# The bias of the second up projection: from a TensorE product to four fused VectorE passes

## The chip, the cores and the metric

The kernel runs on one core of one Trainium2 chip. The metric is the device time of one launch in microseconds, the median of several executions. Three executions of the kernel before took 1491.62, 1492.84 and 1496.29 us; the median is 1492.84 us.

## What is computed

The reference takes x, 8 batches of 512 tokens by 256 channels in fp32, normalises it, and adds to x the outputs of two branches that read the same normalised tokens. One is attention with 16 heads of 16 channels: compressed blocks of 16 tokens, the 4 best blocks of each query, and a window of 32 tokens, merged with a gate. The other is the one at issue here, a gated MLP with 1,024 hidden channels and, beside it, a mixture of 1,024 small experts:

```
mlp = silu(h @ Wg + bg) * (h @ Wu + bu) @ Wd + bd
return mlp + experts_states
```

The gate projection `h @ Wg + bg` is called g below, the second up projection `h @ Wu + bu` is called u. Both biases are random numbers of spread 0.7, in fp32.

## The kernel before

There are four stages, each a block in which the five engines run their own programs and meet at semaphores. The first (until about 24 us) loads weights and prepares them. The second (until about 185 us) normalises and projects all batches. The third, from 187.7 to 1438 us, holds nearly all of the time. The fourth adds the output projection and stores.

The third stage handles 32 units, a unit being one batch and one group of 4 heads. For the attention a unit covers all 512 tokens of its heads; for the MLP and the experts it covers 128 of the batch's 512 tokens. `steps` (a loop over pairs of units, then the last two by hand) calls `step(t)` on every engine. The order within a step is written out by hand for each engine, and the step of unit t already does the first part of unit n = t + 1: its query products, its best blocks and its expert scores. Only the last unit (the tail) has no n.

PSUM banks are dealt out as rings (class `Banks`): Q has two banks for query products (lc, p03, p00, p01, p13, p10, p11, p23, p20, p21, p33, p30, p31, m0, m1 in that order; p11 is head 1, row tile 1 of the n unit), K three banks, F two banks (w0, w1, sim, g0, u0, g1, u1, t0, t1), Y one. A job can be written once the job two places ahead of it in a ring of two has been read. So p11 waits until p13 has been read, and p21 until p23 has been.

Around the change, TensorE's step has this order. `token_rows` gives w0, w1 and sim (line 1625). `up_rows` (lines 1607 to 1620) makes the hidden channels for 128 tokens, transposed: 4 slices of 128 channels for each of g0, u0, g1 and u1. Ahead of the first slice of each job it multiplies the stationary `bias3` (96 rows, bf16) with `tile_of` (96x512, a pattern of ones) into the whole bank (line 1612); the fp32 bias stands in `bias3` as three bf16 terms, in rows 0 to 31, 32 to 63 and 64 to 95. The slices then accumulate on it (line 1617). g0 stands ahead of the four head rounds; then in rounds h = 0, 1, 2 one slice each of u0, g1 and u1 follows each of the four parts, interleaved with `queries(n, h, part)` (line 1635) and the key products. In round 3 come the four parts of `mlp_down` (line 1766), of which parts 0 and 2 wait until u0 and u1 have been read.

ScalarE turns g into a tanh (line 1275), and so w0 and w1; its exponentials are on lines 1241 and 1259. VectorE's step has this order: expert products (line 1495) and `expert_silu` (line 1506), `compressed`, `best_blocks` (line 1413), half of `selection` (line 1438), `gate(0)` (line 1378), the reductions of head 0's query products (`block_max`, line 1394), the other half of `selection`, `up(0)` (line 1385), `best_keys` (line 1467), the reductions of head 1, `key_marks` (line 1475), `gate(1)`, the reductions of head 2, `unselected` (line 1445), `best_pairs`, `up(1)`, the reductions of head 3, and then the local scores and the results. `best_blocks` hands over to GpSimd (line 1120), which hands back. GpSimd sums the expert weights (line 1175) and makes the table of score sums (line 1149).

`bias3` is prepared in the first stage: six small transfers on ScalarE's queue (line 410, three for each bias) into b1, and six VectorE passes (lines 392 to 397). SP loads the weights of the third stage at the end of the second (lines 563 to 567), the last being the bias bdb; behind it SP issues the first qf, kc and xt (line 573). TensorE and GpSimd begin the third stage with a wait for all of these weights (`units_in`).

Of the kernel before, what the change touches and what calls it, by code (L numbers as in the profile page):

```python
# [20 lines left out]
BF16 = mybir.dt.bfloat16  # L21
ALU = mybir.AluOpType
# [7 lines left out]
P = 128  # L30
# [5 lines left out]
FT = FF // P  # L36
# [116 lines left out]
def build(nc, x, Wq, Wk, Wv, Wo, Wck, Wcv, Wg, bg, Fg, fbg, Fu, fbu, Fd, fbd, Rq, keys, down, up, out):  # L153
# [16 lines left out]
    with outer:  # L170
# [11 lines left out]
        sb, ps, sem = make(outer)  # L182
# [11 lines left out]
        wfg = sb("wfg", [P, 2, FF])  # L194
        wfu = sb("wfu", [P, 2, FF])
# [3 lines left out]
        wsim = sb("wsim", [P, 2, 2 * PH * KEYS])  # L199


        bias3 = sb("bias3", [96, 2, 2, P], BF16)
        tile_of = sb("tile_of", [96, 4, P], BF16)
        bdb = sb("bdb", [P, C])
        wo = sb("wo", [P, 2, C])
        ar0 = sb("ar0", [P, TT, C])

        pad = sb("pad", [P, 12])
        units_in = sem("units_in")
# [4 lines left out]
        xt = sb("xt", [P, 2, 2, P])  # L214
# [4 lines left out]
        sb, _, _ = make(projecting)  # L219
# [41 lines left out]
        with inner:  # L261
            sb, ps, sem = make(inner)
# [4 lines left out]
            kn = sb("kn", [P, 2, P])  # L267
            kT = sb("kT", [64, 2, C])
            dn = sb("dn", [P, EX // P, C])
            b1 = sb("b1", [96, 2, 2, P])  # L270
            b2 = sb("b2", [96, 2, 2, P])
            b3 = sb("b3", [96, 2, 2, P], BF16)
            b4 = sb("b4", [96, 2, 2, P], BF16)
            bank = [ps(f"sbank{i}", [P, 512]) for i in range(4)]
            wq_in, rq_in, kn_in, dn_in = sem("wq_in"), sem("rq_in"), sem("kn_in"), sem("dn_in")
            wg_in, bias_in, proj_in = sem("wg_in"), sem("bias_in"), sem("proj_in")
            cleared = sem("cleared")
# [24 lines left out]
            @block.gpsimd  # L302
            def _(pool):
                ch = Chain(pool, pool_chain, 0)
                g = nc.gpsimd

                def keep(ap, pattern, base, cm, fill, op=ALU.is_ge):
                    ch.link(g.affine_select(out=ap, in_=ap, compare_op=op, fill=fill, base=base,
                                            pattern=pattern, channel_multiplier=cm))
                g.memset(eps[:, :], 1e-5)  # L310
                g.memset(b1[:, :, :, :], 0.0).then_inc(cleared, 1)
                for k, m in enumerate((ident, identb)):
                    ch.link(g.memset(m[:, :], 0.0))
                    g.affine_select(out=m[:, :], in_=m[:, :], compare_op=ALU.not_equal, fill=1.0, base=0,
                                    pattern=[[-1, P]], channel_multiplier=1).then_inc(identity, 1)
                    g.memset((wck, wcv)[k][:, :, :], 0.0).then_inc(cleared, 1)
                for m in (any_ok, head_rows):
                    g.memset(m[:], 1.0)
                ch.link(g.memset(quad_rows[:, :], 1.0))
                keep(any_ok[:, :], [[P, TT]], -BLK, 1, 0.0)  # L320
                for rows in (slice(0, 64), slice(64, 128)):
                    keep(head_rows[rows, :], [[-D, HG]], 0, 1, 0.0)
                    keep(head_rows[rows, :], [[D, HG]], D - 1, -1, 0.0)
                keep(quad_rows[:, :], [[-32, HG]], 0, 1, 0.0)
                keep(quad_rows[:, :], [[32, HG]], 31, -1, 0.0)
                g.memset(causal_ts[:, :], 0.0)
                ch.link(g.memset(causal_st[:, :], 0.0))
                keep(causal_ts[:, 0:64], [[-1, 64]], 0, 1, NEG)
                keep(causal_st[:, :], [[1, 64]], 0, -1, NEG)
# [52 lines left out]
            @block.vector  # L382
            def _(dve):
                ch = Chain(dve, dve_chain, 0)
                v = nc.vector
                statistics(dve, 0)
                dve.wait_ge(std_ready, 1)
                ch.link(v.reciprocal(rstd[:, 0, :], std[:, 0, :]))
                normalize(0)
                statistics(dve, 1)  # L390
                dve.wait_ge(bias_in, 6 * 16)
                ch.link(v.tensor_copy(b3[:, :, :, :], b1[:, :, :, :]))
                v.tensor_copy(bias3[0:32, :, :, :], b3[0:32, :, :, :])
                ch.link(v.tensor_tensor(b2[:, :, :, :], b1[:, :, :, :], b3[:, :, :, :], ALU.subtract))
                ch.link(v.tensor_copy(b4[:, :, :, :], b2[:, :, :, :]))
                v.tensor_copy(bias3[32:64, :, :, :], b4[32:64, :, :, :])
                v.tensor_tensor(bias3[64:96, :, :, :], b2[64:96, :, :, :], b4[64:96, :, :, :], ALU.subtract)
                statistics(dve, 2)
                statistics(dve, 3)
                dve.wait_ge(std_ready, 2)  # L400
                v.reciprocal(rstd[:, 1:4, :], std[:, 1:4, :])

            @block.scalar
            def _(act):
                for h in range(8):
                    act.dma_start(wg8[16 * h:16 * h + 16, :], Wg).then_inc(wg_in, 16)
                act.wait_ge(cleared, 1)
                for r in range(3):
                    for a, src in enumerate((fbg, fbu)):
                        act.dma_start(b1[32 * r:32 * r + 4, a, :, :],  # L410
                                      src.rearrange("(j k p) -> k j p", j=2, k=4)).then_inc(bias_in, 16)

                def copy(dst, src, **kw):
                    return nc.scalar.activation(dst, src, ACT.Copy, **kw)
                deviation(act, 0, 1)
                for i, job in enumerate(jobs):
                    b = bank[i % 4]
                    act.wait_ge(pe_full, i + 1)
                    if job[0] == "wqT":
                        last = copy(wqT[:, job[1], :], b[:, 0:C])  # L420
                    elif job[0] == "rqT":
                        last = copy(rqT[:, 2 * job[1]:2 * job[1] + 2, :], b[0:64, :].rearrange("p (k n) -> p k n", k=2))
                    elif job[0] == "kT":
                        last = copy(kT[:, :, :], b[0:64, :].rearrange("p (k n) -> p k n", k=2))
                    elif job[0] == "dn":
                        last = copy(wdn[:, job[1], job[2] * 512:job[2] * 512 + 512], b[:, :])
                    elif job[0] == "wgate":
                        last = copy(wv[:, :, C:C + 3], b[:, 0:8].rearrange("p (a n) -> p a n", a=2)[:, :, 0:3], scale=1.0 / H)
                    else:
                        last = copy(wsim[:, job[1], :], b[:, :])  # L430
                    last.then_inc(read, 1)
                deviation(act, 1, 4)
# [3 lines left out]
        with inner:  # L436
# [69 lines left out]
            def _(sp):  # L506
# [55 lines left out]
                for i in range(B - 4, B):  # L562
                    t = Turn(i // 2, i % 2, tail=(i == B - 1))
                    step(t, None if t.tail else t.next())
                    for dst, src in lots[i]:
                        sp.dma_start(dst[:, :, :], src.rearrange("(a p) n -> p a n", p=P)).then_inc(units_in, 16)
                sp.dma_start(bdb[:, :], fbd.rearrange("(o n) -> o n", o=1).broadcast_to([P, C])).then_inc(units_in, 16)
                for name in ("xt", "qf"):
                    sems, per = by_half[name]
                    sp.wait_ge(sems[0], per * (B // 2 + 1))  # L570
# [312 lines left out]
        with inner:  # L883
# [116 lines left out]
            def hidden(j):  # L1000
                return hT[:, 4 * j:4 * j + 4, :].rearrange("p f t -> p (f t)")
# [90 lines left out]
            def _(pool):  # L1092
# [15 lines left out]
                pool.sem_inc(armed, 1)  # L1108
                pool.wait_ge(constants, 8)

                pool.wait_ge(units_in, 16 * 6)

                def pad_wait():

# [249 lines left out]
            def _(dve):  # L1364
# [16 lines left out]
                def up(t, j):  # L1381

                    F.wait_read(dve, t, f"g{j}")
                    F.wait_full(dve, t, f"u{j}")
                    F.released(f"u{j}", v.tensor_tensor(hidden(j), hidden(j),
                                                        F.bank(f"u{j}")[:, :], ALU.mult))

                def block_max(t, h, part):

# [211 lines left out]
            def _(pe):  # L1601
                mm, tr = nc.tensor.matmul, nc.tensor.transpose
                pe.wait_ge(armed, 1)
                pe.wait_ge(units_in, 16 * 6)
                pe.wait_ge(constants, 8)

                def up_rows(t, name, j, k):

                    w_, kind = (wfg, 0) if name == "g" else (wfu, 1)
                    if k == 0:  # L1610
                        F.wait_free(pe, t, f"{name}{j}")
                        mm(F.bank(f"{name}{j}")[:, :], bias3[:, kind, j, :], tile_of[:, :, :].rearrange("r k t -> r (k t)"),
                           start=True, stop=True)
                    o = P * (4 * j + k)
                    dst = F.bank(f"{name}{j}")[:, k * P:k * P + P]
                    for c in range(2):
                        last = mm(dst, w_[:, c, o:o + P], xt[:, t.half, c, :], start=False, stop=(c == 1),  # L1617
                                  skip_group_check=True)
                    if k == 3:
                        F.filled(f"{name}{j}", last)  # L1620
# [349 lines left out]
```

## Time and profile before

| | |
|---|---|
| median of 3 executions | 1492.84 us (1491.62 to 1496.29) |
| profiled execution, its own time | 1490.08 us |
| its span, first to last instruction | 1488.3 us |
| busy: TensorE matmuls | 1399.5 us (94%) |
| busy: TensorE weight loads | 1041.1 us (70%) |
| busy: VectorE | 1148.8 us (77%) |
| busy: ScalarE | 927.1 us (62%) |
| busy: GpSimd | 946.8 us (64%) |
| mean granted TensorE clock | 0.981 of full speed |

The profile is of one execution. In it PE is TensorE's matmuls, PEld its weight loads, DVE VectorE, ACT ScalarE, POOL GpSimd, SPq the queue of SyncE. A line of a timeline has the start and the length in us, the engine, the source line, the operation, what it writes and what it reads; in brackets stands how long the engine was idle just before, and which engine's work ended that. Lines that follow each other with the same work are merged (x4 is four instructions). Lengths of neighbours overlap, since one instruction begins while the one ahead still ends; what an instruction costs its engine is the distance from its start to the next one's.

### The profile page before, as it was taken

How to read it: one execution, taken by the hardware profiler on the slowest of the kernel's cores; microseconds unless marked ns; L12 is line 12 of the kernel's file. 1: busy time of each engine (PE TensorE's matmuls, PEld its weight loads, DVE VectorE, ACT ScalarE, POOL GpSimd, SP SyncE). 2: the span in 40 equal slices, each digit the busy share in tenths (PEclk: the TensorE clock that was granted, in tenths of full speed). 3: DMA queues.
4: the chain of work that ended last, by engine and by line, in shares of the span. 5: the costliest groups of instructions: out<-in, count | busy, mean ns of one | idle time of the engine just before them, and what ended most of it. 6: DMA issues, size and time to landing. Idle time of an engine off the chain costs nothing. (4 is left out here: it accounts for less than half of the span.)

```text
span 1488.3 us, 43616 instructions
## 1 busy us (share of the span) xinstructions
PE 1399.5 (94%) x14864; PEld 1041.1 (70%) x14960; DVE 1148.8 (77%) x4512; ACT 927.1 (62%) x1684; POOL 946.8 (64%) x877
## 2 busy tenths in 40 slices
PE   6899569999999999999999999999999999999978
PEld 4566437777777777777777777777777777777757
DVE  5444378888888888888888888888888888888712
ACT  3776436666666666666666666666666666666641
POOL 4655357777777766666666666666676666666720
PEclk8999969999999999999999999999999999999989
DMA  6556842211112222222212222122222222222027
GB/s 187 202 192 213 269 82 54 52 44 48 46 47 51 52 52 52 52 50 47 47 47 47 50 52 47 48 52 52 52 52 52 52 52 52 66 52 53 9 83 250
DMA packets 217149, 113.76 MB, mean 76 GB/s; under 512 B 128872, under 2 KB 211224, under 8 KB 217112
## 3 DMA queue, kind: packets, MB, share of 16 engines
q1 hardware_dynamic: 216304, 112.88, 27.9%
q10 hardware_dynamic: 808, 0.42, 0.2%
q8 instruction: 19, 0.31, 0.1%
q14 instruction: 18, 0.15, 0.0%
HBM read 73.08 MB, written 40.16 MB: 76 GB/s over the span
## 5 line engine op out<-in xcount | busy, mean ns | idle before, releaser
L1394 DVE TENSOR_REDUCE bmax<-q_bank 128x32 f32<-128x512 f32 (+3 forms) x512 | 221.2, 487 | 34.4 <-PE q_bank L1635 34.2
L1149 POOL TENSOR_TENSOR sumxy<-xy 128x1024 f32<-128x1024 f32 x128 | 246.1, 1942 | 0.0
L1241 ACT ACTIVATE pts<-k_bank 128x512 f32<-128x512 f32 (+2 forms) x384 | 177.4, 490 | 42.2 <-PE k_bank L1670 41.4
L1115 POOL TENSOR_TENSOR pad<-pad 128x1 f32<-128x1 f32 x32 | 6.2, 193 | 287.4 <-DVE top L1413 287.4
L1495 DVE SCALAR_TENSOR_TENSOR mw<-sumxy,c,ex 128x1024 f32<-128x1024 f32 x128 | 162.0, 1287 | 13.4 <-ACT ex L1259 9.6
L1617 PE MATMUL f_bank<-xt,wfu 128*128 128x128 f32 x1024 | 162.4, 281 | 0.0
L1635 PE MATMUL q_bank<-ko,qo 96*128 96x512 bf16 (+3 forms) x512 | 142.6, 306 | 16.9 <-DVE bmax L1394 16.7
L1175 POOL TENSOR_TENSOR cw<-cw,mw 128x1024 f32<-128x1024 f32 x64 | 150.9, 2358 | 11.5 <-ACT mw L1265 8.9
L1617 PE MATMUL f_bank<-xt,wfg 128*128 128x128 f32 x1024 | 150.3, 279 | 0.0
L1617 PEld LDWEIGHTS f_bank<-xt,wfu 128*128 128x128 f32 x1024 | 139.4, 191 | 11.5
L1318 ACT ACTIVATE oT<-k_bank 128x512 f32<-128x512 f32 x64 | 38.2, 597 | 173.8 <-PE k_bank L1685 129.3
L1265 ACT ACTIVATE mw<-mw,erec 128x1024 f32<-128x1024 f32 x128 | 145.7, 1139 | 0.0
L1259 ACT ACTIVATE ex<-sumxy,nmax 128x1024 f32<-128x1024 f32 x128 | 143.2, 1146 | 0.0
L1617 PEld LDWEIGHTS f_bank<-xt,wfg 128*128 128x128 f32 x1024 | 134.4, 191 | 8.3
L1766 PE MATMUL y_bank<-wfd,hT 128*128 128x256 f32 x512 | 136.0, 388 | 0.5 <-issue 0.5
L1780 PE MATMUL y_bank<-wup,cwT 128*128 128x256 f32 x512 | 124.4, 386 | 8.0 <-ACT cwT L1355 8.0
L1625 PE MATMUL f_bank<-wdn,xt 128*128 128x512 f32 x256 | 122.0, 599 | 0.0
L1309 ACT ACTIVATE qo<-k_bank 32x512 bf16<-32x512 f32 x128 | 75.4, 589 | 60.8 <-PE k_bank L1756 57.9
L1780 PEld LDWEIGHTS y_bank<-wup,cwT 128*128 128x128 f32 x512 | 92.1, 190 | 25.5 <-ACT cwT L1355 15.6
L1766 PEld LDWEIGHTS y_bank<-wfd,hT 128*128 128x128 f32 x512 | 87.2, 190 | 14.4 <-issue 0.7
L1670 PE MATMUL k_bank<-qo,ko 128*128 128x384 bf16 (+3 forms) x416 | 96.0, 280 | 0.0
L1275 ACT ACTIVATE sw<-f_bank 128x512 f32<-128x512 f32 x64 | 38.2, 597 | 79.1 <-PE f_bank L1625 79.0
(211 smaller groups left out, 3307.8 us busy)
## 6 DMA issues: line engine op xcount, KB each, us to landing
qo<-s_qs SPq DMA_DIRECT2D x192, 64.0 KB, 2.2
ko<-s_ks SPq DMA_DIRECT2D x186, 64.0 KB, 2.2
s_qs<-parts SPq DMA_DIRECT2D x8, 768.0 KB, 4.7
s_ks<-parts SPq DMA_DIRECT2D x8, 768.0 KB, 6.3
s_v<-vo SPq DMA_DIRECT2D x8, 544.0 KB, 3.0
vv<-s_v SPq DMA_DIRECT2D x32, 136.0 KB, 2.3
vw<-s_v SPq DMA_DIRECT2D x64, 68.0 KB, 2.5
xin<-in_L_attn_x_dram SPq DMA_DIRECT2D x8, 512.0 KB, 7.1
```

Source lines behind the costliest of these rows:

```text
L1149: done("sum_done", g_.tensor_tensor(sumxy[:, h, :, :], xy[:, 0, h, 0:XK, None].broadcast_to([P, XK, KEYS]), xy[:, 1, h, None, :].broadcast ...
L1175: done("cw_sum", g_.tensor_tensor(cw[:, :], mw[:, 0, :] if h == 1 else cw[:, :], mw[:, h, :], ALU.add))
L1241: last = s.activation(pts[:, h, OFFS[j]:OFFS[j] + n], bank[:, 0:n], ACT.Exp)
L1259: done("ex_done", s.activation(ex[:, h % 2, :], sumxy[:, h, :, :].rearrange("p a b -> p (a b)"), ACT.Exp, bias=nmax[:, h:h + 1]))
L1265: done("ms_done", s.activation(mw[:, h, :], mw[:, h, :], ACT.Copy, scale=erec[:, h:h + 1], accum_out=csm[:, h:h + 1]))
L1394: last = v.tensor_reduce(bmax[:, i, h, 0:n], Q.bank(job)[:, o:o + n * BLK].rearrange("p (n j) -> p n j", j=BLK), AX.X, ALU.max)
L1495: done("mw_done", v.scalar_tensor_tensor(mw[:, h, :], sumxy[:, h, :, :].rearrange("p a b -> p (a b)"), c8[:, h, 7:8], ex[:, h % 2, :], ALU ...
L1617: last = mm(dst, w_[:, c, o:o + P], xt[:, t.half, c, :], start=False, stop=(c == 1), skip_group_check=True)
L1625: last = mm(F.bank(job)[:, :], xt[:, t.half, c, :], w_[:, c, o:o + 512], start=(c == 0), stop=(c == 1))
L1635: last = mm(bank[:, o:o + n], qo[0:SP3, t.half, h, P * i:P * i + P], ko[0:SP3, t.half, h, 0:n], start=True, stop=(i > 0))
L1766: mm(Y.bank("y")[:, 0:C], hT[:, f, :], wfd[:, f, :], start=(f == 0), stop=False)
L1780: last = mm(Y.bank("y")[:, 0:C], cwT[:, e, :], wup[:, e, :], start=False, stop=(e == 7))
```

## The change

The bias of u is no longer a product of TensorE. `up_rows` issues the product of line 1612 for g alone, and for u the first slice product sets the start flag. The bias is kept as bias_u, 128 partitions by 8, one value for each hidden channel, and VectorE's `up(j)` adds it while it multiplies: four scalar_tensor_tensor passes of 128 columns, (bank + bias_u) * hT, take the place of one tensor_tensor pass of 512 columns. `bias3` and its four work tensors lose the half that held u's bias, and so three of the six transfers on ScalarE's queue go. bias_u is loaded by one transfer on SP's queue, behind bdb and ahead of qf, kc and xt, and `units_in` is waited for at 7 transfers instead of 6.

```diff
-        bias3 = sb("bias3", [96, 2, 2, P], BF16)
+        bias3 = sb("bias3", [96, 2, P], BF16)
+        bias_u = sb("bias_u", [P, FT])
...
-                dve.wait_ge(bias_in, 6 * 16)
-                ch.link(v.tensor_copy(b3[:, :, :, :], b1[:, :, :, :]))
+                dve.wait_ge(bias_in, 3 * 16)
+                ch.link(v.tensor_copy(b3[:, :, :], b1[:, :, :]))
...
                 for r in range(3):
-                    for a, src in enumerate((fbg, fbu)):
-                        act.dma_start(b1[32 * r:32 * r + 4, a, :, :],
-                                      src.rearrange("(j k p) -> k j p", j=2, k=4)).then_inc(bias_in, 16)
+                    act.dma_start(b1[32 * r:32 * r + 4, :, :],
+                                  fbg.rearrange("(j k p) -> k j p", j=2, k=4)).then_inc(bias_in, 16)
...
+                sp.dma_start(bias_u[:, :], fbu.rearrange("(f p) -> p f", p=P), allow_slow_non_contiguous=True).then_inc(units_in, 16)
...
-                pool.wait_ge(units_in, 16 * 6)
+                pool.wait_ge(units_in, 16 * 7)
...
                     F.wait_full(dve, t, f"u{j}")
-                    F.released(f"u{j}", v.tensor_tensor(hidden(j), hidden(j),
-                                                        F.bank(f"u{j}")[:, :], ALU.mult))
+                    for k in range(4):
+                        f = 4 * j + k
+                        last = v.scalar_tensor_tensor(hT[:, f, :], F.bank(f"u{j}")[:, P * k:P * k + P], bias_u[:, f:f + 1],
+                                                      hT[:, f, :], ALU.add, ALU.mult)
+                    F.released(f"u{j}", last)
...
-                pe.wait_ge(units_in, 16 * 6)
+                pe.wait_ge(units_in, 16 * 7)
...
-                    w_, kind = (wfg, 0) if name == "g" else (wfu, 1)
+                    w_ = wfg if name == "g" else wfu
                     if k == 0:
                         F.wait_free(pe, t, f"{name}{j}")
-                        mm(F.bank(f"{name}{j}")[:, :], bias3[:, kind, j, :], tile_of[:, :, :].rearrange("r k t -> r (k t)"),
+                    if k == 0 and name == "g":
+                        mm(F.bank(f"{name}{j}")[:, :], bias3[:, j, :], tile_of[:, :, :].rearrange("r k t -> r (k t)"),
                            start=True, stop=True)
...
-                        last = mm(dst, w_[:, c, o:o + P], xt[:, t.half, c, :], start=False, stop=(c == 1),
+                        last = mm(dst, w_[:, c, o:o + P], xt[:, t.half, c, :], start=(name == "u" and c == 0), stop=(c == 1),
                                   skip_group_check=True)
```

## Rows read from the trace of the kernel before

**Rows 1.** Busy time of each engine in stretches of the third stage: TensorE, weight loads, VectorE, ScalarE, GpSimd, clock, DMA
```profile
260.00:1380.00 1120.00, 1097.61 (x12671) 819.72 (x12759) 958.60 (x3882) 740.10 (x1405) 770.69 (x701) 1.00 0.21 50
716.94:734.46 17.52, 17.18 (x131) 13.90 (x132) 16.83 (x98) 15.43 (x32) 9.96 (x9) 1.00 0.17 32
```

**Rows 2.** Timeline of TensorE's matmuls, one unit (start us, length us, idle time ahead)
```profile
712.72 1.88 PE L1625 MATMUL f_bank<-wdn,xt 128*128 128x512 f32 x4
...
723.20 0.38 PE L1612 MATMUL f_bank<-tile_of,bias 96*128 96x512 bf16 x1
723.42 0.61 PE L1617 MATMUL f_bank<-xt,wfu 128*128 128x128 f32 x4
...
730.20 0.28 PE L1635 MATMUL q_bank<-ko,qo 96*128 96x256 bf16 x1 [0.23 <-DVE bmax L1394]
...
731.93 0.38 PE L1612 MATMUL f_bank<-tile_of,bias 96*128 96x512 bf16 x1
...
739.96 1.03 PE L1766 MATMUL y_bank<-wfd,hT 128*128 128x256 f32 x4
```

**Rows 3.** The same view, product p11 in an early and in a late unit
```profile
269.59 0.28 PE L1635 MATMUL q_bank<-ko,qo 96*128 96x256 bf16 x1 [0.24 <-DVE bmax L1394]
...
1152.56 0.28 PE L1635 MATMUL q_bank<-ko,qo 96*128 96x256 bf16 x1 [0.25 <-DVE bmax L1394]
```

**Rows 4.** Table of waits from 260 to 1380 us (us in total, times, longest)
```profile
PE q_bank L1635 <- DVE bmax L1394: 7.0, 29, 0.3
```

**Rows 5.** Timeline of TensorE's weight loads, product p21 of the same unit
```profile
734.50 0.10 PEld L1635 LDWEIGHTS q_bank<-ko,qo 96*128 96x128 bf16 x1 [0.15 <-DVE bmax L1394]
```

**Rows 6.** Timeline of ScalarE, the same unit
```profile
714.72 0.60 ACT L1275 ACTIVATE sw<-f_bank 128x512 f32<-128x512 f32 x1 [2.54 <-PE f_bank L1625]
```

**Rows 7.** Timeline of VectorE, the same unit
```profile
713.09 0.42 DVE L1528 SCALAR_TENSOR_TENSOR yo<-y_bank,xb 128x256 f32<-128x256 f32 x1 [0.89 <-PE y_bank L1780]
713.43 2.47 DVE L1495 SCALAR_TENSOR_TENSOR mw<-sumxy,c,ex 128x1024 f32<-128x1024 f32 x2
715.82 0.68 DVE L1506 SCALAR_TENSOR_TENSOR sw<-sw,f_bank 128x512 f32<-128x512 f32 x1
716.94 1.28 DVE L1495 SCALAR_TENSOR_TENSOR mw<-sumxy,c,ex 128x1024 f32<-128x1024 f32 x1 [0.44 <-ACT ex L1259]
...
727.84 0.69 DVE L1385 TENSOR_TENSOR hT<-hT,f_bank 128x512 f32<-128x512 f32 x1
728.45 0.22 DVE L1467 MAX8 t<-sim 128x8 f32<-128x64 f32 x1
...
729.47 1.67 DVE L1394 TENSOR_REDUCE bmax<-q_bank 128x32 f32<-128x512 f32 x4
...
733.76 1.68 DVE L1394 TENSOR_REDUCE bmax<-q_bank 128x32 f32<-128x512 f32 x4
...
738.00 0.67 DVE L1385 TENSOR_TENSOR hT<-hT,f_bank 128x512 f32<-128x512 f32 x1
...
740.05 0.76 DVE L1394 TENSOR_REDUCE bmax<-q_bank 128x8 f32<-128x128 f32 x2 [0.73 <-PE q_bank L1635]
```

**Rows 8.** Timelines of SP's queue and of TensorE where the third stage begins
```profile
179.78 1.26 SPq L567 DMA_DIRECT2D bdb<-in_L_ffn_bd_dram  x1
...
182.40 0.60 SPq L573 DMA_DIRECT2D xt<-s_xt  x1
...
187.68 2.04 PE L1728 MATMUL q_bank<-kc,qf 64*128 64x128 f32 x8 [11.68 <-DMA xt<-s_xt]
```

**Rows 9.** Timelines of VectorE and GpSimd, passes side by side
```profile
214.30 3.24 DVE L1495 SCALAR_TENSOR_TENSOR mw<-sumxy,c,ex 128x1024 f32<-128x1024 f32 x2 [0.89 <-issue]
...
735.35 1.97 DVE L1445 TENSOR_SCALAR unsel<-struck 128x512 bf16<-128x512 f32 x1
...
726.17 2.36 POOL L1175 TENSOR_TENSOR cw<-cw,mw 128x1024 f32<-128x1024 f32 x1
...
735.13 3.94 POOL L1149 TENSOR_TENSOR sumxy<-xy 128x1024 f32<-128x1024 f32 x2
```

More of the change, by code:

```diff
@@ L269, in build @@
             dn = sb("dn", [P, EX // P, C])
[L270 to L273, printed above, removed]
+            b1 = sb("b1", [96, 2, P])
+            b2 = sb("b2", [96, 2, P])
+            b3 = sb("b3", [96, 2, P], BF16)
+            b4 = sb("b4", [96, 2, P], BF16)
             bank = [ps(f"sbank{i}", [P, 512]) for i in range(4)]
@@ L310, in _ @@
                 g.memset(eps[:, :], 1e-5)
-                g.memset(b1[:, :, :, :], 0.0).then_inc(cleared, 1)
+                g.memset(b1[:, :, :], 0.0).then_inc(cleared, 1)
                 for k, m in enumerate((ident, identb)):
@@ L390, in _ @@
                 statistics(dve, 1)
-                dve.wait_ge(bias_in, 6 * 16)
-                ch.link(v.tensor_copy(b3[:, :, :, :], b1[:, :, :, :]))
[L393 to L397, printed above, removed]
+                dve.wait_ge(bias_in, 3 * 16)
+                ch.link(v.tensor_copy(b3[:, :, :], b1[:, :, :]))
+                v.tensor_copy(bias3[0:32, :, :], b3[0:32, :, :])
+                ch.link(v.tensor_tensor(b2[:, :, :], b1[:, :, :], b3[:, :, :], ALU.subtract))
+                ch.link(v.tensor_copy(b4[:, :, :], b2[:, :, :]))
+                v.tensor_copy(bias3[32:64, :, :], b4[32:64, :, :])
+                v.tensor_tensor(bias3[64:96, :, :], b2[64:96, :, :], b4[64:96, :, :], ALU.subtract)
                 statistics(dve, 2)
```

## The prediction

> **What bounds the kernel now.** I looked for the stage first. In the stretch of the third stage in which every unit is alike, TensorE's matmuls cover 1,097.6 of 1,120 us and VectorE is busy for 958.6, at a granted clock of 1.00, which is 2.4 GHz [rows 1]. Read alone, that says: TensorE is the bound, so a matmul taken away is time gained. The timeline of one unit shows how far that holds. The same small wait returns in every unit: the last query product of head 1 (p11) stands 0.23 to 0.25 us until VectorE has read a bank [rows 2, 3], and the table of waits counts it 29 times in 29 units, 7.0 us in all [rows 4]. From the first of these waits shown to the last are 23 units: (1152.56 - 269.59) / 23 = 38.39 us a unit [rows 3]. One product later in the same ring, p21, the weight load waits 0.15 us on VectorE again [rows 5].
>
> So I followed that wait backwards. TensorE writes w0 from 712.72 on; ScalarE, idle for 2.54 us until it comes, takes it at 714.72 [rows 2, 6]. VectorE waits 0.44 us for ScalarE's exponential at 716.94, and from there to the end of the reduction that frees p21's bank (733.76 + 0.69) it is busy for 16.83 of 17.52 us [rows 1, 7]; what is left is mostly one hand-over to GpSimd and back. In that stretch stand the first up product (727.84), the eight maxima behind it (728.45) and the reduction of p13 (729.47, four reductions), which frees the bank that p11 wants [rows 7]. **TensorE and VectorE run side by side from w0 to p21, and VectorE arrives last.** From p21 to the next w0 TensorE is alone the limit: VectorE itself idles there, 0.73 us ahead of the reduction at 740.05 [rows 7]. A unit is thus VectorE's half plus TensorE's half.
>
> **Part one, the bias product is gone (u0 and u1).** 2 in each of 32 units, 64 in all. Start to start it takes 723.42 - 723.20 = 0.22 us [rows 2]; its busy time is longer since matmuls overlap. 64 x 0.22 = 14.1 us if TensorE were the limit at both places. But both stand between w0 (712.72) and p21 (734.50): at 723.20 and at 731.93 [rows 2, 5]. There TensorE already arrives early and waits. What it saves is added to its waits at p11 and p21. I take 0 for the 31 units with a successor; the last has no query products and no such wait, and may give back 2 x 0.22 = 0.4 us. The start flag set on each 128 columns' first matmul instead adds no instruction.
>
> **Part two, the up product as four passes.** The one pass of 512 columns takes 728.45 - 727.84 = 0.61 us start to start [rows 7]. No row shows a pass of 128 columns with one operand in PSUM and a per-partition scalar, so I build it. The result pass (256 columns, same instruction, PSUM source, constant scalar) takes 713.43 - 713.09 = 0.34 us start to start; 256 columns at 0.96 GHz are 0.267, which leaves 0.07 fixed. The expert pass has a per-partition scalar and 1,024 columns: (715.82 - 713.43) / 2 = 1.195 us, less 1.067 for its columns is 0.128 [rows 7]. The scalar so seems to cost 0.055 more. A new pass is 0.133 + 0.07 + 0.055 = 0.26 us, four are 1.05 us, and **VectorE needs 0.44 us more for each up product**. Bounds: 4 x 0.20 = 0.81 if the scalar is free (+0.20), and 4 x 0.30 = 1.20 if each pass pays 0.04 more yet (+0.59). I take the middle value because the two rows it comes from are the same instruction.
>
> The Trainium skill (VectorE: DVE Perf Modes, section on the TRN2 errata) speaks against small tiles too: a pass pays its fixed latency each time, (N + 151) / 0.96 ns for an fp32 pass of N columns. Laid end to end that would be 4 x 291 - 691 ns = +0.47 us a product, an estimate from that page, and 0.9 us more over the kernel than my sum; the rows agree with the direction, but show the next pass starting before the last one's end.
>
> Where the two extra 0.44 us fall: the first (up of u0, at 727.84) lies ahead of the p13 reduction, inside VectorE's chain. Everything behind it moves by 0.44: p11, key marks, the reduction at 733.76, p21. This is paid whole, 31 x 0.44 = 13.6 us. The second (at 738.00) lies behind p21. Behind it wait the reduction of p33 and the second half of the down product (part 2, at 739.96), which reads its result; that product would be written at about 738.00 + 0.67 + 0.88 = 739.55 while part 2 itself has moved to 740.4, and VectorE's idle 0.73 us takes the rest [rows 2, 7]. Cost 0, with 0.8 us of cover; without that cover it would be another 13.6 us.
>
> **Part three, the prologue.** Three bias transfers fewer on ScalarE's queue and six VectorE conversions of half the width: all end before a wait for input data in the first 25 us, so 0 (at best -1 us). New is one transfer of bias_u, 1,024 single elements, issued on SP's queue between bdb and the first qf, kc and xt. The bdb issue took 1.26 us (179.78); xt was issued at 182.40 and TensorE's first product of the stage began at 187.68, after 11.68 us of waiting that ended with xt [rows 8]. Whatever the issue takes moves xt, and both TensorE and GpSimd also wait for bias_u itself. Nearest row: an issue like bdb's, +1.3 us; bounds 0 (the stage change hides it) and +5 (it lands late in a busy queue). I take 1.3. The Trainium skill (DMA: Bandwidth & Descriptors, Rules for kernel authors) says a transfer whose last dimension is not contiguous becomes one descriptor per element; no row here shows such a transfer.
>
> **Sum.** +13.6 + 1.3 - 0.4 = +14.5 us. The profiled execution took 1490.08 us, the median of the runs shown is 1492.84, 0.2% more; I add the sum to the median: **1507.3 us**, 1.0% slower. A difference below 0.3% (4.5 us) can't be told from none.
>
> **The rivals.**
> *A. TensorE is the bound after all.* Its 98% speaks for it, the wait in every unit against it: an engine that waits for another at p11 doesn't profit from work taken away before p11. It would give 1492.8 - 14.1 + 1.3 = 1480 us, faster. It decides if VectorE's chain has slack that the wait doesn't show, at least 0.44 us. Chance 0.07.
> *B. Half and half.* The p21 wait of 0.15 us is small, so the second bias product might still count, with VectorE's extra at its low bound: 31 x (0.20 - 0.22) + 1.3, about 0: 1493 to 1495 us. Chance 0.07.
> *C. GpSimd blocks the new passes.* VectorE does get stuck behind GpSimd: a 512-column pass over SBUF took 1.97 us at 735.35 beside a GpSimd product of 735.13, and the expert pass, which takes 1.19 elsewhere, took some 2.0 of the 3.24 at 214.30. The up product with one side in PSUM isn't held today: 0.67 to 0.69 us, at 727.84 beside GpSimd's sum from 726.17 to 728.53 [rows 7, 9]. The new passes read a second SBUF operand, the scalar. If that counts, the first pass waits 0.7 us and a later one for the next sum of 2.36: 31 x (0.7 + 0.44) = +35 us at least, 31 x 3.5 = +108 at most; 1529 to 1600 us. The Trainium skill (SBUF — State Buffer, Who interferes with whom) says a VectorE instruction with two SBUF inputs contends with a GpSimd one that reads SBUF; whether a [P, 1] scalar is such an input it doesn't say. Chance 0.06.
>
> **Numbers.** Forecast 0.80. Its own range: 31 x 0.20 = 6.2 and 31 x 0.59 = 18.3, with 0 to 5 us of prologue: 1499 to 1516. B lies just below, A and C outside; the range 1497 to 1517 leaves out a little under 2 in 10. Faster by over 0.3% 0.08, within 0.07, slower 0.85.
>
> **What would show each step.** Right: a new pass of about 0.34 us busy, 0.26 start to start; the p11 wait at 0.23 + 0.22 + 0.44 = 0.9 us and p21's at 0.15 + 0.22 = 0.37; 38.83 us a unit; VectorE's wait at 740.05 down from 0.73 to 0.3. Wrong: a unit shorter than 38.39 (A), up passes of unequal length beside GpSimd (C), a wait for u1's result at the down product's part 2, or TensorE's first product of the stage more than 5 us later. A clock below 1.00 with the longer waits would be a cost that I don't count.

## The result and the profile after

The changed kernel took 1506.61 us, the median of 4 executions (1504.32 to 1510.04), against 1492.23 us for the kernel before beside it: a ratio of 1.0097, 95% interval 1.0075 to 1.0119, which is 14.4 us or 1.0% slower. The forecast was 1507.3 us. The profiled execution has a span of 1508.3 us and is the slowest of the four, 1510.04 us; the others took 1504.32 to 1507.10. So the difference of the two profiled spans, 20.0 us, is not the measure of the change. In the traces, the stretch in which all units are alike is a better one.

TensorE in the changed kernel, by the timeline: the product p11 in an early, two middle and a late unit, and the work ahead of and behind u0's first slice (line 1622 is line 1617 of before, 1640 is 1635, 1678 is 1673).

```profile
276.83 0.28 PE L1640 MATMUL q_bank<-ko,qo 96*128 96x256 bf16 x1 [1.01 <-DVE bmax L1398]
...
704.49 0.28 PE L1640 MATMUL q_bank<-ko,qo 96*128 96x256 bf16 x1 [0.82 <-DVE bmax L1398]
...
735.80 0.19 PE L1678 MATMUL k_bank<-causal_st,identb 128*128 128x64 bf16 x1
735.83 0.69 PE L1622 MATMUL f_bank<-xt,wfu 128*128 128x128 f32 x4
736.36 0.38 PE L1640 MATMUL q_bank<-ko,qo 96*128 96x512 bf16 x1
...
743.37 0.28 PE L1640 MATMUL q_bank<-ko,qo 96*128 96x256 bf16 x1 [0.91 <-DVE bmax L1398]
...
1171.00 0.28 PE L1640 MATMUL q_bank<-ko,qo 96*128 96x256 bf16 x1 [0.81 <-DVE bmax L1398]
```

From the first to the last are 23 units: (1171.00 - 276.83) / 23 = 38.88 us a unit, where it was 38.39 [rows 3]. The wait at p11 has grown from 0.24 us to 0.81 or 0.82 in every second unit and 0.90 to 0.92 in the others (1.01 in the first). TensorE has less to do and takes longer: 31 x 0.49 = 15 us.

VectorE in the same kernel: the first up product, what stands behind it, the second one and the reductions of p33 and p30 (line 1388 is 1385 of before, 1398 is 1394, 1471 is 1467).

```profile
740.56 1.13 DVE L1388 SCALAR_TENSOR_TENSOR hT<-f_bank,bias_u,hT 128x128 f32<-128x128 f32 x4 [0.23 <-DVE struck L1442]
741.61 0.22 DVE L1471 MAX8 t<-sim 128x8 f32<-128x64 f32 x1
...
742.63 1.67 DVE L1398 TENSOR_REDUCE bmax<-q_bank 128x32 f32<-128x512 f32 x4
...
751.16 1.11 DVE L1388 SCALAR_TENSOR_TENSOR hT<-f_bank,bias_u,hT 128x128 f32<-128x128 f32 x4
752.18 0.68 DVE L1398 TENSOR_REDUCE bmax<-q_bank 128x32 f32<-128x512 f32 x1
753.21 0.76 DVE L1398 TENSOR_REDUCE bmax<-q_bank 128x8 f32<-128x128 f32 x2 [0.35 <-PE q_bank L1640]
```

Four passes take 741.61 - 740.56 = 1.05 us where one took 0.61 [rows 7]: the 0.44 us more of the forecast. The idle time ahead of p30's reduction has shrunk from 0.73 to 0.35 us: there the second product's extra time has gone, at no cost. All 256 passes of the kernel are alike, 329 to 353 ns (shortest, median and longest in ns below), although GpSimd is busy for most of that stretch:

```profile
L1388 DVE SCALAR_TENSOR_TENSOR hT<-f_bank,bias_u,hT x256: 329/341/353, 235.1 to 1445.8; 128x128 f32<-128x128 f32 x128
```

The second wait, at p21, seen on the weight load, is 0.28 us, where it was 0.15 [rows 5]:

```profile
747.66 0.10 PEld L1640 LDWEIGHTS q_bank<-ko,qo 96*128 96x128 bf16 x1 [0.28 <-DVE bmax L1398]
```

Where the third stage begins, by SP's queue and TensorE's timeline (to be read beside [rows 8]):

```profile
184.71 0.81 SPq L567 DMA_DIRECT2D bdb<-in_L_ffn_bd_dram  x1
185.57 0.44 SPq L568 DMA_DIRECT2D bias_u<-in_L_ffn_bu_dram  x1
186.12 1.66 SPq L574 DMA_DIRECT2D qf<-s_qf  x1
...
188.47 0.60 SPq L574 DMA_DIRECT2D xt<-s_xt  x1
...
193.91 2.04 PE L1733 MATMUL q_bank<-kc,qf 64*128 64x128 f32 x8 [11.68 <-DMA xt<-s_xt]
```

The stage begins 6.2 us later than in the profile of before, and most of that is not the change's: bdb, ahead of the new transfer, was issued 4.9 us later already. From bdb to xt it is 3.76 us against 2.62: the transfer of 1,024 single elements moves xt by 1.1 us. Its own issue takes 0.44 us; the one behind it, qf, is the slow one (1.66 us, where it took 0.56 before). From bdb to TensorE's first product it is 9.20 us against 7.90, 1.3 us more.

The traces of the twelve experiments below show that this pair isn't typical. In the seven kernels with the transfer bdb to xt takes 3.2 to 4.4 us (mean 3.9), in the seven without 2.2 to 2.7 (mean 2.6), so that xt is 1.3 us later. But bdb to the first product takes 8.4 us in the mean with it and 8.1 without: most of the delay is hidden. The first product also waits for GpSimd, which clears the tile vw at the start of the stage, and in seven of the fourteen traces the profile puts its wait down to that, as in the third experiment:

```profile
192.93 2.04 PE L1738 MATMUL q_bank<-kc,qf 64*128 64x128 f32 x8 [10.25 <-POOL vw L1109]
```

The stage's start itself lies between 186.8 and 193.1 us without the transfer and between 188.4 and 193.9 with it: it varies by some 6 us from run to run for another reason, which was not looked for.

### The profile page after: what moved, and what is told of

The parts are those of the page before. It is cut to its first block and busy times, and to the rows that moved or that the text cites. A ratio compares the mean times of both kernels' runs of the same rounds, so it can differ in the third digit from the quotient of the medians.

```text
span 1508.3 us, 43678 instructions
## 1 busy us (share of the span) xinstructions
PE 1397.7 (93%) x14800; PEld 1041.9 (69%) x14896; DVE 1174.3 (78%) x4704; ACT 924.0 (61%) x1684; POOL 946.2 (63%) x877
## 5 line engine op out<-in xcount | busy, mean ns | idle before, releaser
L1622 PE MATMUL f_bank<-xt,wfu 128*128 128x128 f32 x1024 | 167.7, 286 | 0.0
L1622 PEld LDWEIGHTS f_bank<-xt,wfu 128*128 128x128 f32 x1024 | 134.2, 191 | 17.3
L1640 PEld LDWEIGHTS q_bank<-ko,qo 96*128 96x128 bf16 x512 | 50.4, 99 | 58.4 <-DVE bmax L1398 54.2
```

Of the source, the lines that this page charges most:

```text
L1640: last = mm(bank[:, o:o + n], qo[0:SP3, t.half, h, P * i:P * i + P], ko[0:SP3, t.half, h, 0:n], start=True, stop=(i > 0))
```

## The experiments

The theory says that VectorE's path from w0 to p21 sets the time of that half of a unit. The rivals are that TensorE's sum does, or VectorE's sum, or half of each. In the first four the changed kernel is taken apart, all beside the same executions of the kernel before (median 1491.28 us). The kernels of 5 to 8 ran beside others of it (1493.16 us), and so did 9 and 10 (1492.70) and 11 and 12 (1492.65). The edits are against the kernel before, in 7, 10 and 12 against the changed one, and shortened where "..." stands.

**1. The product out, the pass as before.** The kernel leaves out the bias of u; the start flag moves to u's first slice product.

```diff
                     if k == 0:
                         F.wait_free(pe, t, f"{name}{j}")
+                    if k == 0 and name == "g":
                         mm(F.bank(f"{name}{j}")[:, :], bias3[:, kind, j, :], tile_of[:, :, :].rearrange("r k t -> r (k t)"),
...
-                        last = mm(dst, w_[:, c, o:o + P], xt[:, t.half, c, :], start=False, stop=(c == 1),
+                        last = mm(dst, w_[:, c, o:o + P], xt[:, t.half, c, :], start=(not (name == "g") and c == 0), stop=(c == 1),
```

> The kernel before without the 64 bias products of u, the up pass as it was; the bias of u is left out. Chain theory (VectorE arrives last at p11 and p21): the products' time goes into TensorE's waits; 38.39 us a unit as before, the p11 wait grows from 0.24 to 0.45 us, the time changes by 0 to -1 us. Rival, TensorE is the bound: -0.22 us at each product, 37.95 us a unit, -14 us (ratio 0.991).

Measured: 1492.08 us, ratio 1.0001 (0.9988 to 1.0013). TensorE, by its timeline:

```profile
270.92 0.28 PE L1636 MATMUL q_bank<-ko,qo 96*128 96x256 bf16 x1 [0.38 <-DVE bmax L1394]
...
724.53 0.19 PE L1674 MATMUL k_bank<-causal_st,identb 128*128 128x64 bf16 x1
724.56 0.69 PE L1618 MATMUL f_bank<-xt,wfu 128*128 128x128 f32 x4
725.08 0.38 PE L1636 MATMUL q_bank<-ko,qo 96*128 96x512 bf16 x1
...
1153.85 0.28 PE L1636 MATMUL q_bank<-ko,qo 96*128 96x256 bf16 x1 [0.39 <-DVE bmax L1394]
```

(1153.85 - 270.92) / 23 = 38.39 us a unit: 64 products taken away from an engine that is busy 98% of the time are worth nothing. The waits took them: p11's grew from 0.24 to 0.38 us, by 0.14 and not by 0.22, and p21's, on the weight load, from 0.15 to 0.29. In the rows the first slice and what leads to it take 725.08 - 724.53 = 0.55 us, where with the product they took 0.70 (723.17 to 723.87 in the trace of before). So the product was worth 0.14 to 0.15 us to TensorE. The weight loads show where the rest went. Before, those of u0's first slice begin at 723.21 us, under the product of 723.20, and the slice's own products at 723.42, 0.21 later. Here loads (724.53) and products (724.56) begin together, and the four products take 725.08 - 724.56 = 0.52 us start to start, where they took 723.87 - 723.42 = 0.45:

```profile
723.21 0.63 PEld L1617 LDWEIGHTS f_bank<-xt,wfu 128*128 128x128 f32 x4
...
724.53 0.53 PEld L1618 LDWEIGHTS f_bank<-xt,wfu 128*128 128x128 f32 x4
```

**2. The passes in, the product kept.** Their scalar is a tile of zeros that GpSimd fills in the second stage.

```diff
...
-                    F.released(f"u{j}", v.tensor_tensor(hidden(j), hidden(j),
-                                                        F.bank(f"u{j}")[:, :], ALU.mult))
+                    for k in range(4):
+                        f = 4 * j + k
+                        last = v.scalar_tensor_tensor(hT[:, f, :], F.bank(f"u{j}")[:, P * k:P * k + P], bias_u[:, f:f + 1],
+                                                      hT[:, f, :], ALU.add, ALU.mult)
+                    F.released(f"u{j}", last)
```

> The kernel before with the bias product kept and the up product as four fused passes, their scalar a tile of zeros, so that the computation is the same; no transfer is added. Chain theory: 38.83 to 38.88 us a unit, +13.6 to +15 us, the same as with the whole change but for the prologue, since the removed products are worth nothing; the p11 wait is 0.7 us. Rival, the change's cost is VectorE's 0.44 less TensorE's 0.22: this kernel would be 7 us slower than the whole change, +21 us. Rival, all of VectorE's extra time counts (2 x 0.44 a unit): +27 us less what the idle 0.73 us takes.

Measured: 1509.88 us, ratio 1.0110 (1.0092 to 1.0129), 38.87 us a unit. With or without the products it is the same unit, to 0.01 us. The whole loss is VectorE's.

**3 and 4. The change for u0 alone, and for u1 alone** (there with 1 in the place of both 0). bias_u is loaded as in the changed kernel.

```diff
...
                     F.wait_full(dve, t, f"u{j}")
-                    F.released(f"u{j}", v.tensor_tensor(hidden(j), hidden(j),
-                                                        F.bank(f"u{j}")[:, :], ALU.mult))
+                    if j == 0:
+                        for k in range(4):
...
+                        F.released(f"u{j}", last)
+                    else:
+                        F.released(f"u{j}", v.tensor_tensor(hidden(j), hidden(j),
+                                                            F.bank(f"u{j}")[:, :], ALU.mult))
...
                         F.wait_free(pe, t, f"{name}{j}")
+                    if k == 0 and (name, j) != ("u", 0):
...
```

> The change for u0 alone: its product gone, its up product as four passes; u1 keeps its product and its one pass; bias_u is loaded as in the change. Chain theory: the first up product carries the whole cost, 38.83 to 38.88 us a unit, +13.6 us and 1 us of prologue (ratio 1.010). Rival, each of the two costs half: +7 to +8 us (ratio 1.005).

> The change for u1 alone. Chain theory: VectorE's extra 0.44 us lies behind p21, where it idles 0.73 us, and the product that is gone lies ahead of p21, where TensorE waits: 38.39 us a unit, +1 us from the prologue (ratio 1.000 to 1.001); VectorE's wait ahead of p30's reduction falls from 0.73 to 0.3 us. Rival, each of the two costs half: +7 us. Rival, TensorE's bound: -7 us.

Measured: u0 alone 1508.10 us, ratio 1.0098 (1.0078 to 1.0118), 38.83 us a unit; u1 alone 1491.55 us, ratio 1.0000 (0.9988 to 1.0013), 38.40 us a unit. The same edit costs everything at one place and nothing at the other, and the rivals that share the cost are gone. In the kernel with u1 alone VectorE does spend the time: 740.82 - 739.79 = 1.03 us for the four, where the one pass took 0.63 (738.00 to 738.63 in the trace of before). It idles 0.40 us less for it, 0.33 instead of 0.73:

```profile
739.79 1.11 DVE L1390 SCALAR_TENSOR_TENSOR hT<-f_bank,bias_u,hT 128x128 f32<-128x128 f32 x4
740.82 0.68 DVE L1403 TENSOR_REDUCE bmax<-q_bank 128x32 f32<-128x512 f32 x1
741.83 0.76 DVE L1403 TENSOR_REDUCE bmax<-q_bank 128x8 f32<-128x128 f32 x2 [0.33 <-PE q_bank L1645]
```

**5. Four passes without the scalar**, `v.tensor_tensor(hT[:, f, :], hT[:, f, :], F.bank(f"u{j}")[:, P * k:P * k + P], ALU.mult)`, the products kept.

> The kernel before, bias products kept, each up product as four tensor_tensor passes of 128 columns with no per-partition scalar. Theory of the price: a pass has 0.07 us fixed beside its 0.133, four take 0.81 us, +0.20 a product; only the first product of a unit counts, 38.59 to 38.63 us a unit, +6 to +8 us (ratio 1.004 to 1.005). Rival: the scalar is free and every pass has 0.13 us fixed, 1.05 us for four, the same as with the change, +14 us (ratio 1.010).

Measured: 1500.27 us beside 1493.16, ratio 1.0048 (1.0035 to 1.0062), 38.64 us a unit.

```profile
732.50 0.88 DVE L1387 TENSOR_TENSOR hT<-hT,f_bank 128x128 f32<-128x128 f32 x4 [0.23 <-DVE struck L1440]
733.31 0.22 DVE L1469 MAX8 t<-sim 128x8 f32<-128x64 f32 x1
```

Four take 0.81 us. Cutting one pass in four costs 0.20 us, and what the new passes have beyond these costs (1.05 - 0.81) / 4 = 0.06 us a pass: a little over half of the 0.44 isn't the cutting. These passes differ from the new ones in the instruction as well as in the scalar, but the instruction is not it. `gate` in the trace of before is a scalar_tensor_tensor over the same two operands with a constant scalar, and takes 733.76 - 733.16 = 0.60 us, as the tensor_tensor does (0.61):

```profile
733.16 0.68 DVE L1378 SCALAR_TENSOR_TENSOR hT<-hT,f_bank 128x512 f32<-128x512 f32 x1
```

The unit grows by 0.25 us and not by 0.20; the last section has the other 0.05.

**6 and 7. VectorE's order changed, in the kernel before and in the changed one.** If VectorE's path to p21 sets the time, work that p11 and p21 don't need can go behind them.

```diff
                     up(t, 0)
                     if n:
-                        best_keys(n)
                         for part in range(3):
                             block_max(n, 1, part)
+                        best_keys(n)
                     expert_sum(t)
-                    if n:
-                        key_marks(n)
                     gate(t, 1)
                     if n:
                         for part in range(3):
                             block_max(n, 2, part)
+                        key_marks(n)
```

> The kernel before with two pieces of VectorE's work put behind the reductions that free the banks: the eight maxima of the scores (1.02 us) behind head 1's reductions, the key marks and their mask (2.0 us) behind head 2's. Nothing is added or removed. Chain theory: the waits at p11 (0.24) and p21 (0.15) go, the unit is TensorE's own, 38.0 us, -12 us (ratio 0.992). Rival: another wait takes their place, GpSimd gets the mask 2 us later and its sums hold up VectorE's best pairs or TensorE's transposes, and less than half of it or nothing is gained.

> The whole change with the same two pieces moved. Chain theory: with VectorE no longer last at p11 and p21, the removed products become worth their 0.14 us each (measured in the trace of the first experiment; not 0.22), VectorE's passes nothing: 37.72 us a unit, -20 us with 1 us of prologue (ratio 0.987), 8 to 9 us faster than the kernel before so reordered. The sign of the change turns with the order of the work around it. Rival: the 0.44 us still costs somewhere, and this one is slower than the kernel before so reordered, at 38.0 to 38.4 us a unit.

Measured: 1513.81 us, ratio 1.0143 (1.0125 to 1.0161), and 1514.25 us, ratio 1.0145 (1.0126 to 1.0165), 39.15 and 39.08 us a unit. Both expectations miss, and by more than the rivals said: the kernels are slower than the kernel before and not only short of a gain. GpSimd's timeline in the sixth:

```profile
708.02 1.38 POOL L1144 TENSOR_TENSOR xy<-xy,sim 128x512 f32<-128x512 f32 x1 [4.54 <-DVE xy L1477]
...
724.18 1.71 POOL L1193 TENSOR_TENSOR at<-on,co 128x256 f32<-128x256 f32 x1
```

VectorE's, with the best pairs and the first expert passes:

```profile
710.02 0.22 DVE L1483 MAX8 c<-cand 128x8 f32<-128x64 f32 x1 [1.75 <-issue]
...
723.21 3.76 DVE L1495 SCALAR_TENSOR_TENSOR mw<-sumxy,c,ex 128x1024 f32<-128x1024 f32 x2
```

And TensorE's:

```profile
711.26 1.13 PE L1765 MATMUL y_bank<-wfd,hT 128*128 128x256 f32 x4 [0.46 <-DVE hT L1385]
```

GpSimd waits 4.54 us for the mask, where it waited 1.49. VectorE then stands for 1.75 us. The trace names no releaser, but the candidates that it reads next are GpSimd's, written from 709.36 to 709.98, and it goes on at 710.02. The second up product is queued behind, and TensorE's down product waits 0.46 us for that. And GpSimd's work of the unit's end now lies beside VectorE's expert passes: two of them take 3.76 us instead of 2.47 [rows 7], and GpSimd's 256-column sum 1.71 instead of 0.73. The wait at p11 did go, but p21's grew: on the weight load it is 0.53 us, where it was 0.15. How the 0.76 us a unit divide between these causes, no run shows. In the seventh p21's is 0.28 and the down product waits 0.91. What was moved away from one wait was handed on to another.

**8. The second up product's cover, used up.** As the fourth (the lines with - are its), with 16 passes of 32 columns.

```diff
-                        for k in range(4):
-                            f = 4 * j + k
+                        for k in range(16):
+                            f, o = 4 * j + k // 4, 32 * (k % 4)
...
```

> As the experiment with the change for u1 alone, but with 16 passes of 32 columns. A pass is 0.033 + 0.13 us, the product 2.6 us instead of 1.05. It ends 0.8 us after the down product's third part wants it. Chain theory: the second up product is free only as long as its cover of some 0.8 us lasts; the unit becomes 39.1 to 39.3 us, +22 to +27 us (ratio 1.015 to 1.018), with a wait of 0.6 to 0.9 us ahead of the third part. Rival: VectorE's work behind p21 never counts, and the time stays that of the kernel before.

Measured: 1517.02 us, ratio 1.0159 (1.0140 to 1.0179), 39.18 us a unit. TensorE waits ahead of the down product's third part. VectorE's timeline, and TensorE's:

```profile
712.36 2.61 DVE L1390 SCALAR_TENSOR_TENSOR hT<-f_bank,bias_u,hT 128x32 f32<-128x32 f32 x16
714.88 1.34 DVE L1403 TENSOR_REDUCE bmax<-q_bank 128x32 f32<-128x512 f32 x3
```

```profile
715.02 1.13 PE L1776 MATMUL y_bank<-wfd,hT 128*128 128x256 f32 x4 [0.52 <-DVE hT L1390]
```

The sixteen cost VectorE 714.88 - 712.36 = 2.52 us start to start, 1.49 more than the four of the fourth, and 0.78 of it are paid (39.18 - 38.40). The other 0.71 were cover, which the prediction had taken as 0.8 us.

**9 and 10. An order that hands GpSimd the mask as early as before.** Head 1's reductions ahead of best_keys; gate 1 behind head 2's; then best_pairs, the second up product, unselected, head 3's.

```diff
-                        best_keys(n)
                         for part in range(3):
                             block_max(n, 1, part)
+                        best_keys(n)
                     expert_sum(t)
                     if n:
                         key_marks(n)
-                    gate(t, 1)
-                    if n:
                         for part in range(3):
                             block_max(n, 2, part)
+                    gate(t, 1)
                     if n:
-                        unselected(n, now=t)
                         best_pairs(n)
                     up(t, 1)
                     if n:
+                        unselected(n, now=t)
                         for part in range(3):
                             block_max(n, 3, part)
```

> The kernel before with another order on VectorE, which hands the mask to GpSimd no later than today: head 1's reductions ahead of the eight maxima (1.02 us), gate 1 (0.60 us) behind head 2's reductions, and behind it the best pairs, the second up product, and only then the unselected blocks (1.97 us, most of it spent waiting for GpSimd) and head 3's reductions. Nothing is added or removed. Chain theory: p11 and p21 no longer wait, 38.0 us a unit, -12 us (ratio 0.992). Rival: as in the last reordering, VectorE meets GpSimd somewhere else and the gain is lost to it.

> The whole change with that same order. Chain theory: TensorE is now the bound, the two removed products are worth 0.14 us each and VectorE's extra 0.88 us lies in its idle time: 37.7 us a unit, -20 us with 1 us of prologue (ratio 0.986 to 0.988), 7 to 9 us faster than the kernel before in the same order. Rival: the extra passes still cost 0.44 us a unit, 38.0 to 38.4 us, not faster than the kernel before in the same order.

Measured: kernel before in this order 1489.20 us, ratio 0.9973 (0.9960 to 0.9987), 38.28 us a unit; changed kernel 1490.09 us, ratio 0.9983 (0.9971 to 0.9995), 38.35 us a unit. Both expectations miss. The ninth gains 0.11 us a unit where 0.39 was expected; the tenth was expected to be 7 to 9 us faster than the ninth and is not faster, as its rival said. In the ninth VectorE stands ahead of p10:

```profile
726.42 0.69 DVE L1394 TENSOR_REDUCE bmax<-q_bank 128x32 f32<-128x512 f32 x1
727.42 1.09 DVE L1394 TENSOR_REDUCE bmax<-q_bank 128x8 f32<-128x128 f32 x3 [0.31 <-PE q_bank L1634]
728.44 0.22 DVE L1467 MAX8 t<-sim 128x8 f32<-128x64 f32 x1
```

It comes to head 1's second reduction before TensorE has written that product. The four reductions take 728.44 - 726.42 = 2.02 us, where they took 1.59 before (729.47 to 731.06): 0.43 of the 0.60 us that the moved gate had won are lost, and with the wait at p11 gone the one at p21 remains, 29 times in the table of waits:

```profile
732.35 0.28 PE L1634 MATMUL q_bank<-ko,qo 96*128 96x256 bf16 x1 [0.25 <-DVE bmax L1394]
```

The changed kernel, 0.44 us later on VectorE, doesn't find that hole (its four take 732.38 - 730.78 = 1.60 us) and is only 0.07 us a unit longer than the ninth. Its wait at p21 is 0.58 us.

**11 and 12. The maxima in the hole.** As 9 and 10, with best_keys between p13's reduction and the other ones of head 1. Here the diff is against 9 and 10.

```diff
-                        for part in range(3):
-                            block_max(n, 1, part)
+                        block_max(n, 1, 0)
                         best_keys(n)
+                        for part in range(1, 3):
+                            block_max(n, 1, part)
```

> The kernel before in the order of the ninth experiment, but with the eight maxima between head 1's first reduction (p13, which frees p11's bank) and its other ones. In the ninth VectorE stood 0.31 us ahead of p10, which TensorE had not written yet; the maxima fill that hole. Chain theory: VectorE's path to p21 is 0.60 us shorter than in the kernel before and needs only 0.39; both waits go, TensorE is the bound, 38.0 us a unit, -12 us (ratio 0.992). Rival: a path through GpSimd sets 38.28 us in the ninth experiment, and this one stays there.

> The whole change in the same order. Chain theory: VectorE's path to p21 is 0.44 us longer than in the eleventh and TensorE's 0.28 shorter; 0.60 - 0.39 = 0.21 us of room is left for the 0.44, so VectorE stays the bound, 38.2 to 38.3 us a unit, -4 to -6 us (ratio 0.996 to 0.997), 6 to 8 us slower than the kernel before in this order. Rival: the change now gains its 0.28 us a unit, 37.7 us, and is the fastest of all.

Measured: kernel before in this order **1476.33 us, ratio 0.9890 (0.9873 to 0.9907)**, 37.85 us a unit; changed kernel 1488.90 us, ratio 0.9976 (0.9966 to 0.9986), 38.29 us a unit. Table of waits from 262 to 1380 us (in total, times, longest) for the eleventh, all of TensorE's waits for VectorE, and for the twelfth the one at p21:

```profile
PE k_bank L1673 <- DVE hT L1385: 5.1, 30, 0.2
```

```profile
PE q_bank L1640 <- DVE bmax L1398: 14.9, 30, 0.5
```

In the eleventh no query product waits any more. The 0.17 us that are left at k_bank are nothing new: in the trace of before the same product stands idle as long, with no releaser shown (`PE k_bank L1673 <- issue: 5.1, 29, 0.2`). So VectorE no longer sets the unit, and TensorE's own sequence does, but for one short hand-over to ScalarE and back ahead of the expert product (line 1780), which all these kernels have:

```profile
PE y_bank L1780 <- ACT cwT L1355: 7.2, 29, 0.3
```

The eleventh gained 0.54 us a unit, more than the 0.39 that its two waits seemed to add to. At p11 the idle time in brackets is less than what is lost: the step from the slice ahead of it, 729.37 in the trace of before, to 730.20 is 0.83 us, and for head 0's like product 0.45 (725.20 to 725.65), so 0.38 for a wait shown as 0.23. At p21 the step is 734.50 - 733.93 = 0.57, so 0.12. Together they are 0.50 of the 0.54. The change put into this order costs 38.29 - 37.85 = 0.44 us a unit again, 12.6 us by the medians, and came out as expected.

## Why the prediction held

- *VectorE's path from w0 to p21 sets the time of that half.* Shown three ways: the products taken out are worth nothing (1), the passes alone cost all of it (2), and putting other work of VectorE's behind the same waits makes the kernel 1.1% faster with nothing removed (11). That from p21 on TensorE is "alone the limit" leaves out its wait for ScalarE, 7.2 us in 29 units in the kernel before as in the eleventh, as much as p11's; the change touches neither side of it.
- *0.44 us a product.* Measured 1.05 - 0.61 = 0.44; its parts, 0.07 fixed and 0.055 for the scalar, measured (0.81 - 0.61) / 3 = 0.07 and 0.06 (5).
- *The first product counts whole, the second not at all.* 0.44 and 0.01 us a unit (3, 4). The second's cover is there and is finite: what exceeds the four passes by more than 0.7 us is paid (8).
- *The removed product is worth 0 here.* Right, but the 0.22 us that it was said to take was mis-sized, and with it rival A: TensorE gets 0.14 us back for each, so even as the bound it would have gained 9 us, not 14. For the same reason the p11 wait came to 0.24 + 0.14 + 0.44 = 0.82 us and not 0.9 (the 0.91 of every second unit is this and the 0.10 of the last section), and p21's to 0.28 and not 0.37. No run showed the 0.14 us as time gained in the units that have a successor: in no order tried was TensorE the bound there with the change in.
- *The last unit gives back 0.4 us.* From the last p11 to the start of the stage's last expert products it is 1435.63 - 1382.79 = 52.84 us before and 52.02 both in the changed kernel and in the first experiment: 0.8 us, twice the forecast. Why was not looked for.
- *The prologue at +1.3 us.* The first product of the stage comes 1.3 us later behind bdb in this pair, but only 0.3 us later in the mean of the fourteen traces, though xt is 1.3 us later: the bound of 0, that the stage change hides it, is nearer. It is too small for the medians to show.
- *GpSimd doesn't block the new passes.* Right for them, with a longest of 353 ns among 256. That it does hold up VectorE where both read SBUF was rightly read from the trace, and has a part in the sixth run (3.76 us for 2.47).

The mechanism held, and the total is closer than its terms. By the traces the sum is 31 x 0.49 - 0.8 and 0.3 to 1.3 us of prologue, 14.7 to 15.7 us: the forecast had the unit 0.05 us too short, 1.5 us in all, the prologue up to 1 us too long and what the last unit gives back 0.4 us too small. The measured 14.4 us have an interval from 11.2 to 17.8, which holds all of this. That 14.5 and 14.4 agree to 0.1 us is luck.

## What to carry to other kernels

A small wait that returns in every round decides what an edit is worth, not the busy shares: follow it back to where the late engine's path began, and ask of each edit on which side of that wait it lies. Then the cheap test of such a theory is to reorder the late engine's work rather than to shorten it, and here that gave the best kernel. When work is moved past a wait, look at who else receives it (here GpSimd), and whether what comes earlier is already there to be read (here p10).

## What the runs showed that was not expected

- Taking out a matmul of 0.22 us gave TensorE 0.14: it had covered part of the weight load of the fp32 product behind it (1).
- A per-partition scalar costs VectorE 0.06 us in each pass (5), nearly as much as the 0.07 us fixed cost of a pass with one operand in PSUM. A constant one costs nothing that the rows show.
- A transfer of 1,024 single elements takes 0.44 us to issue and makes xt 1.3 us later in the mean of the fourteen traces, but TensorE's first product of the stage only 0.3 us.
- TensorE's idle time ahead of p11 reads 0.23 us and its step there is 0.38 us too long (11).
- In the changed kernel every second unit's first up product starts 0.10 us later (0.42 us behind the start of the selection's last pass, instead of 0.32), shown as a wait on its own engine in 15 of 29 units. It is there where both up products are cut in pieces (2, 5, 7, 10, 12) and not where one is (3, 4). Shared between two units, it is the step from 38.83 to 38.88 us a unit. Its cause was not looked for.
